# A token mixer, cosine attention and mixture of experts on one NeuronCore: pairs of heads attended two at a time, and the fillers of TensorE's order moved

## The reference, cut to what matters

```python
# token mixer, per sample: x is (F=64, L=256, H=4)
q, k, v = proj(Wq), proj(Wk), proj(Wv)             # (256, 256) each
ew = exp(w_bias * local_mask); ek = exp(k)
y = sigmoid(q) * (ew @ (ek * v)) / (ew @ ek)
h = layernorm(y @ out_w + out_b + flatten(x))
# attention over 257 tokens, 16 heads, DK = 16, DV = 64
t = layernorm(h)
q, k, v = l2norm(t @ Wq), l2norm(t @ Wk), l2norm(t @ Wv)    # per head
out = square(relu(q @ k.T)) @ v                    # per head
out = tanh(|out|) * out / |out|                    # per head and token
h = h + concat(out) @ Wout
```

## Time and profile before

| | |
|---|---|
| median of three runs | 3233.44 us (3223.12 to 3235.12) |
| profiled execution, its own time | 3228.84 us |
| its span in the profile | 3227.0 us |
| PE busy | 2987.7 us (93%) |
| DVE, ACT, POOL busy | 2108.6 (65%), 1431.1 (44%), 1150.4 us (36%) |
| loop of the 32 samples | about 100 to 1630 us of the span |

### The profile page before, as it was taken

The page is one execution under the profiler, slowest core; times in us unless marked ns, Lnnn a source line. Parts: engine busy times, 40 slices in busy tenths (PEclk is TensorE's granted clock), DMA queues, the critical chain, the costliest instruction groups (busy, mean ns, idle before and its releaser), DMA issues. The chain is left out here.

```text
span 3227.0 us, 67632 instructions
## 1 busy us (share of the span) xinstructions
PE 2987.7 (93%) x21936; PEld 2303.3 (71%) x21937; DVE 2108.6 (65%) x5558; ACT 1431.1 (44%) x2884; POOL 1150.4 (36%) x973
## 2 busy tenths in 40 slices
PE   3999999999999999999859999999999992999998
PEld 1677777777777777777537777777777761999997
DVE  4677777767777777776526777777777765444443
ACT  0444554554454455445404444444444442444443
POOL 3333433443443344344311222222222224444444
PEclk7999999999999999999969999999999995999999
DMA  3333442443343344234221111111111101444444
GB/s 82 92 87 73 101 99 66 95 104 75 81 104 88 72 101 103 64 92 104 49 51 31 37 49 42 36 52 41 37 52 39 39 31 46 73 75 78 76 78 67
DMA packets 161128, 223.14 MB, mean 69 GB/s; under 512 B 30305, under 2 KB 125730, under 8 KB 161074
## 3 DMA queue, kind: packets, MB, share of 16 engines
q1 hardware_dynamic: 135138, 187.50, 23.2%
q0 software_dynamic: 25936, 34.95, 6.9%
HBM read 125.26 MB, written 97.08 MB: 69 GB/s over the span
## 5 line engine op out<-in xcount | busy, mean ns | idle before, releaser
L66 POOL TENSOR_TENSOR vrn<-vsm,inv_root 128x16 f32<-128x16 f32 x64 | 247.1, 3862 | 282.1 <-DVE vsm L844 282.1
L673 ACT ACTIVATE R<-psA 128x1024 f32<-128x1024 f32 x256 | 262.5, 1025 | 167.9 <-PE psA L1158 164.3
L865 DVE TENSOR_TENSOR PR<-R 128x1024 f32<-128x1024 f32 x256 | 320.9, 1254 | 0.0
L2528 POOL DMA_INDIRECT out_rows<-e_y,e_dest x137 | 213.4, 1557 | 290.7 <-DMA out_rows<-e_y,e_dest 205.8
L1907 DVE TENSOR_REDUCE m_nm<-psC 128x4 f32<-128x1028 f32 (+1 forms) x256 | 239.4, 958 | 99.5 <-PE psC L2184 99.4
L1173 PE MATMUL psA<-PR,V 128*64 128x258 f32 x2048 | 283.2, 397 | 0.0
L1785 ACT ACTIVATE m_PT<-psC 128x770 f32<-128x770 f32 x256 | 194.1, 811 | 150.5 <-PE psC L2210 150.5
L678 ACT ACTIVATE oTs<-psA 128x258 f32<-128x258 f32 x256 | 99.2, 387 | 357.9 <-PE psA L1173 352.3
L1218 PE MATMUL psA<-wout,OT 128*128 128x256 f32 x1024 | 244.5, 382 | 0.4 <-DVE OT L907 0.4
L1704 POOL DMA_INDIRECT xg<-tn,idx x124 | 122.4, 987 | 335.5 <-DMA xg<-tn,idx 225.4
L1218 PEld LDWEIGHTS psA<-wout,OT 128*128 128x128 f32 x1024 | 188.5, 191 | 24.6 <-DVE OT L907 0.7
(11 more groups left out here) (423 smaller groups left out, 7774.4 us busy)
## 6 DMA issues: line engine op xcount, KB each, us to landing
ks<-kparts SPq DMA_DIRECT2D x256, 128.0 KB, 3.2
qs<-qparts SPq DMA_DIRECT2D x256, 128.0 KB, 3.6
e_x<-xg SPq DMA_DIRECT2D x143, 129.0 KB
xraw<-in_x SPq DMA_DIRECT2D x66, 256.0 KB
qparts<-qh SPq DMA_DIRECT2D x128, 128.0 KB, 2.4
kparts<-kh SPq DMA_DIRECT2D x64, 128.0 KB, 2.5
kparts<-kl SPq DMA_DIRECT2D x64, 128.0 KB, 2.4
qparts<-ql SPq DMA_DIRECT2D x64, 128.0 KB, 2.4
```

Of the source, the lines that this page charges most:

```text
L66: return pool.tensor_tensor(out, x, e.to_broadcast(list(out.shape)), ALU.pow)
L673: act.activation(R[:, p % 2].rearrange("p a t n -> p t a n"), ps[:, 0:2, :].rearrange("p t (a n) -> p t a n", a=2), ACT.Relu).then_inc(rel ...
L865: dve.tensor_tensor(PR[:, p % 2, :, :, 0:L], R[:, p % 2], R[:, p % 2], ALU.mult).then_inc(prob_done, 1)
L2528: pool.indirect_dma_start(out, bass.IndirectOffsetOnAxis(ap=dest[:, b % XD:b % XD + 1], axis=0), y[:, b % XD], None, compute_op=ALU.add).t ...
```

## The change

`attend` takes two pairs, `first` and `first + 1`: it waits until the outputs of the two pairs before are taken, adds the class part of both pairs, and then runs the matmuls of both, the second four behind a wait for the second pair's probabilities. So a sample has four visits in place of eight. The orders of TensorE, ACT and DVE are rewritten around that. POOL's and SP's are as before. No operation is added or taken away. DVE's lines have numbers lower by one than before, TensorE's lower by two up to `attend` and higher by one behind it, ACT's are as they were: `mixer_queries` is L1029, `mix_keys` L1043, `mixer_output` L1071, `sim` L1156, the class part L1167, the visit's matmuls L1174, `onm` L884, `mixed_rows` L783.

```diff
@@ attend, TensorE
-            def attend(i, d, p):
-                if p == 0:
+            def attend(i, d, first):
+                pairs = (first, first + 1)
+                if first == 0:
                     pe.wait_ge(p_ready, i + 1)
                     pe.wait_ge(v_ready, 2 * i + 2)
-                need(pe, o_sq, PAIRS * i + p - 1)
-                pe.wait_ge(prob_done, PAIRS * i + p + 1)
-                pe.matmul(ps[:, 2 + p % 2, 0:QCOLS], ...)
-                for t in range(LT):
...
-                last.then_inc(av_done, 1)
+                need(pe, o_sq, PAIRS * i + first)
+                for p in pairs:
+                    pe.matmul(ps[:, 2 + p % 2, 0:QCOLS], ...)
+                for p in pairs:
+                    pe.wait_ge(prob_done, PAIRS * i + p + 1)
+                    for t in range(LT):
...
+                    last.then_inc(av_done, 1)
@@ sample, DVE
                     denominators(j)
                     inverses(j, 0)
-                prob(i, d, 2)
                 if before:
                     output_scale(i - 1, 1 - d)
                 if more:
                     inverses(j, 1)
+                    mixed_rows(j)
+                prob(i, d, 2)
                 if before:
                     output_scale_turned(i - 1)
-                if more:
-                    mixed_rows(j)
+                prob(i, d, 3)
                 if before:
                     split_scale(i - 1)
-                prob(i, d, 3)
```

More of the change, by code:

```diff
@@ L703, in sample @@
                     take_outputs(i - 1, 1 - d, 7)
-                relu(i, 0)
                 if before:
                     sums_out(i - 1, 1)
+                relu(i, 0)
                 if more:
@@ L709, in sample @@
                 relu(i, 1)
-                take_outputs(i, d, 0)
                 relu(i, 2)
-                take_outputs(i, d, 1)
                 if before:
                     norm_tanh(i - 1)
+                take_outputs(i, d, 0)
+                take_outputs(i, d, 1)
                 relu(i, 3)
+                relu(i, 4)
                 take_outputs(i, d, 2)
-                relu(i, 4)
                 take_outputs(i, d, 3)
                 relu(i, 5)
-                take_outputs(i, d, 4)
+                relu(i, 6)
                 sums_out(i, 0)
@@ L725, in sample @@
                     queries(j)
-                    values(j, 0)
-                relu(i, 6)
-                if more:
-                    values(j, 1)
+                take_outputs(i, d, 4)
                 take_outputs(i, d, 5)
@@ L732, in sample @@
                 if more:
+                    values(j, 0)
+                    values(j, 1)
                     values(j, 2)
@@ L1160, in sim @@
                 last.then_inc(sim_done, 1)
-            def attend(i, d, p):
-                if p == 0:
+            def attend(i, d, first):
+                pairs = (first, first + 1)
+                if first == 0:
                     pe.wait_ge(p_ready, i + 1)
                     pe.wait_ge(v_ready, 2 * i + 2)
-                need(pe, o_sq, PAIRS * i + p - 1)
-                pe.wait_ge(prob_done, PAIRS * i + p + 1)
-                pe.matmul(ps[:, 2 + p % 2, 0:QCOLS], v.vcls3[:, p * P:(p + 1) * P], v.pcl[:, d, :], start=True,
-                          stop=False, skip_group_check=True)
-                for t in range(LT):
[L1171 to L1174, removed]
-                last.then_inc(av_done, 1)
+                need(pe, o_sq, PAIRS * i + first)
+                for p in pairs:
+                    pe.matmul(ps[:, 2 + p % 2, 0:QCOLS], v.vcls3[:, p * P:(p + 1) * P], v.pcl[:, d, :], start=True,
+                              stop=False, skip_group_check=True)
+                for p in pairs:
+                    pe.wait_ge(prob_done, PAIRS * i + p + 1)
+                    for t in range(LT):
+                        for hh in range(2):
+                            n = 2 * p + hh
+                            last = pe.matmul(ps[64 * hh:64 * hh + 64, 2 + p % 2, 0:QCOLS], V[:, d, t, n * DV:(n + 1) * DV],
+                                             PR[:, p % 2, hh, t, :], start=False, stop=True, skip_group_check=True)
+                    last.then_inc(av_done, 1)
             def head_sums(i, b):
@@ L1243, in sample @@
                 j = i + 1
-                sim(i, 0)
                 if more:
@@ L1250, in sample @@
                     mixer_keys(j, 0)
+                sim(i, 0)
                 if before:
@@ L1255, in sample @@
                 sim(i, 1)
-                attend(i, d, 0)
                 if more:
@@ L1261, in sample @@
                     mix_values(j)
-                attend(i, d, 1)
+                attend(i, d, 0)
                 if more:
@@ L1265, in sample @@
                 sim(i, 3)
-                attend(i, d, 2)
+                if more:
+                    mixer_output(j)
                 if before:
                     turn_scale(i - 1, more)
-                if more:
-                    mixer_output(j)
                 sim(i, 4)
+                attend(i, d, 2)
                 if before:
@@ L1282, in sample @@
                     project_outputs(i - 1, 2)
-                attend(i, d, 4)
+                sim(i, 6)
                 head_sums(i, 0)
@@ L1292, in sample @@
                     project_queries(j)
[L1293 to L1297, removed]
+                attend(i, d, 4)
                 sim(i, 7)
                 if more:
+                    project_values(j, 0)
+                    project_values(j, 1)
                     key_sums(j)
```

3 lines of the change are left out of this document (removed).

## The result

The changed kernel takes 3274.42 us (median of four runs, 3272.63 to 3279.87) against 3229.13 us of the kernel before on the same chip: a ratio of 1.0143, 95% interval 1.0117 to 1.0169. The forecast was 3278 us, slower. The profiled execution took 3274.26 us; the sum had said 3274 for it.

A forecast was written before the change was run, and what follows sets the result against it. TensorE was taken as the bound, 47.43 us a sample. New waits of 3.45 less gains of 1.94 give +1.51 us per sample, +45 over thirty; against the 3233.44 median, forecast 3278 us, range 3238 to 3312.

The forecast's parts named there:

- query sums directly before the queries: TensorE's mixer queries wait for DVE's q_lift, no longer covered: 0.55 us per sample, bounds 0.3 to 0.6.
- mix of keys: Without the first visit in front, it waits for ACT's exponentials: 0.65 us per sample, bounds 0 and 0.9.
- mixer output: Block L1071 waits for y_done, delayed by POOL's root ahead of the second inverse: 1.9 us per sample, bounds 0.9 to 2.3.
- first output projection: Little is left between it and the spread it needs, so it waits for DVE's L907: 0.35 us, 0 to 0.5.
- class products, behind the key norms: Key norms come 0.2 us before TensorE asks: no cost, up to 0.5 us if late.
- gains, visits and old waits: Fewer visits and class-row places save 1.25 us per sample, vanished old waits 0.69: together 1.94.
- The largest term: The mixer output's wait for y_done behind POOL's 5.42 us root: 1.9 us per sample.
- Rival C: Waits cost only their idle time, weight loads being pulled ahead: +0.47 us per sample, about 3247 us; chance 0.09.
- The 0.43 of waiting: Old order's first class row waits 0.43 us for the first probabilities; goes if the new place covers it.
- B: Faster: y_done comes in time for the mixer output, sample changes by -0.40 to -1.0 us, some 3210; chance 0.10.
- D: Slower still: the new hole lowers TensorE's clock, +1.13 us in each of thirty samples, 3310 us; chance 0.11.
- The lock between DVE and POOL: POOL's 16-row operation starting first might hold DVE's first probabilities: chain up to about 0.4 us longer, sum 12 us.

The follow-up runs named there:

- Experiments 1 and 5: On the changed kernel: 1 moves DVE's output_scale behind the mixed rows, 3244.19 us; 5 replaces POOL's root of the output norms by a multiplication, 3229.56 us.
- experiment 3: The changed kernel with ACT's exponential of the queries ahead of the first relu, behind a DMA wait: 3287.26 us, 1.0174 of the kernel before.

## Why the prediction was right

Term by term, in us per sample; the measured costs are the mean steps of the changed kernel less those of the same block with nothing to wait for:

| term | forecast | measured |
|---|---|---|
| query sums directly before the queries | 0.55 | 0.61 |
| mix of keys | 0.65 | 0.66 |
| mixer output | 1.9 | 1.84 |
| first output projection | 0.35 | 0.35 |
| third output projection | 0 | 0.18 |
| class products, behind the key norms | 0, up to 0.5 | 0.10 |
| gains, visits and old waits | -1.94 | -2.01 (the remainder) |
| sum | +1.51 | +1.73 |

*The largest term* held in its parts. From the end of the turned sums (L1191, 1032.99) osm ended 3.04 later, the root 8.53 and y_done 11.47, where the forecast had 3.04, 8.54 and 11.5; TensorE arrived after 9.97 (forecast 9.95). Experiments 1 and 5 take the root out in two ways, once by order and once by length, and the hole goes with it in both.

*The two small terms that failed* were wrong in their price, not in their place. The key norms were placed 0.2 before TensorE asks, and that is where they came:

```profile
1072.53 0.62 PE L1116 MATMUL psA<-wvh,xl 128*128 128x512 f32 x2
1073.02 1.09 PE L1135 MATMUL psA<-xT,wkc 128*80 128x256 f32 x4
...
1072.78 0.18 DVE L815 TENSOR_SCALAR km<-psA 128x32 f32<-128x32 f32 x1
```

They end at 1072.96, 0.19 before the block in front of the class products ends (1073.15), and the class products still take 0.96 for 0.86. "Nothing" was the wrong price for that. The third projection the forecast did not look at: it priced the first alone. The third waits for DVE's third scaling (L906), which stands in DVE's queue behind the first layer norm of the next sample and the statistics of the second; in the sample above it ended at 1054.63, 0.09 before TensorE was free. Its step is 1.91 for 1.73. Together 0.28, the whole excess of the waits.

*What a signal costs.* These rows give a price that the forecast had only for a signal that is late. Take how long before the end of the block in front DVE's result is finished, and what the block behind loses:

| block | finished before the end in front, us | lost, us |
|---|---|---|
| third projection, kernel before | 0.35 to 0.49 | 0 |
| class products, changed kernel | 0.19 | 0.09 |
| third projection, two kinds of samples | 0.18, 0.10 | 0.14, 0.22 |
| mixer output, experiment 1, two kinds of samples | 0.22, 0.11 | 0.10, 0.21 |
| mixer output, kernel before | 0.06 | 0.26 |
| first projection, changed kernel | -0.03 | 0.35 |
| mixer output, changed kernel | -1.50 | 1.82 |

For the output projections and the mixer output the two add up to 0.32 each time something is lost, for the class products, with 80 stationary columns, to 0.28. So a result has to be there about 0.3 us ahead of TensorE to cost nothing, and a block can lose up to 0.27 without showing any idle time. Where it does show some, the cost is more by 0.27 in the mix of keys, the mixer output and the first projection, and by 0.24 in the queries. The forecast was 0.26.

The page "TensorE: Matmul & The Clock Gate" of the Trainium skill, in the section "Architectural detail: the array is 16× 32×32, not 1× 128×128", says that weight loads can be pulled ahead of matmuls in flight. That did not shorten these waits. In the mixer output and the mix of keys the stationary operand is the late tile itself, so there was nothing to load; in the queries it is wq_bd, which is always there, and still the load starts at 1029.29, 0.11 behind the end of qm. Rival C has fallen.

*The gains*, -2.01 against -1.94, agree better than their parts. The visits are as forecast. The 0.43 of waiting in front of the first class row was read in one sample; over 25 the old kernel waited 0.28 there. What makes up for it was not in the sum: the old order's last similarity had a step of 0.81 in the mean, 0.66 without waits (TensorE stood idle 2.6 us in the 29 periods for the DMA of queries), and its last visit one of 1.09, 1.02 at the full clock.

*Where the total agreed by luck.* 29 periods give +50.1 us, 6 more than 29 times 1.51; the spans differ by 45.2, the 45 of the forecast. Before the first period the changed kernel gains 3.0 (144.49 against 147.50). The first similarity of sample 0 had waited 3.00 us for the DMA of its queries; it now stands behind the mixer's queries and keys and waits 0.74. From the last mark on, over samples 30 and 31, it loses 4.2, where 1.5 was forecast for sample 30 alone. The prediction had put sample 31, which has no mixer, at nothing; but there the turned scale now comes ahead of the third pair of heads and not behind it, and it waits for the same root. The first row is sample 0 in the kernel before, the second sample 31 in the changed one:

```profile
100.12 1.19 PE L1158 MATMUL psA<-qs,ks 128*128 128x512 f32 x2 [3.00 <-DMA qs<-qparts]
```

```profile
1633.07 0.69 PE L1200 MATMUL psA<-ident,osc 128*128 128x128 f32 x2 [4.81 <-DVE osc L893]
```

In the kernel before that second wait was 0.24. All that comes behind, which the change does not touch, took 6.1 us less in this execution; its largest stage takes 1058 to 1069 us over the eleven traces. So errors of +6, -3, +3 and -6 cancelled.

*Rivals.* B needed a signal 1.65 us earlier, and got none. D was not seen here: the loop's granted clock is 1.00, and the longest period is 49.24. But something like it was near: with a hole of 1.88 us in place of 1.54 to 1.63 (experiment 3) the clock fell in five of fifteen samples, at 1.7 us each and not the 1.13 taken.

*The lock between DVE and POOL*, left in the range, did not matter: POOL's 16-row operation ran at 1032.22 in 0.63 us, over by 1032.85, about 1 us before DVE's first probabilities. The class parts had ended earlier than forecast. In the kernel before the two had met in nearly every sample, and where POOL came first DVE's probabilities took 1.76 us and not 1.22: 0.5, a little more than the 0.4 of the forecast's upper bound.

## What to carry to other kernels

When work is taken from between a producer and its consumer, add up what the removed blocks had covered: four visits fewer saved about 2 us of TensorE's time and old waits and uncovered 3.7. In an in-order queue the position of the wait decides, not the position of the work: one wait for a 5.4 us root, put in front of an inverse, cost 1.1 to 1.3 of the 2.0 us gained, and moving four calls, without touching a matmul's count, turned 1.4% slower into 0.5% faster. A moved wait takes its followers along: with output_scale behind the mixed rows the largest hole closed, and 0.5 us came out at the two blocks that hang on output_scale, each to be found in the next trace. And "just in time" is late: a result finished 0.2 us before TensorE was free still cost 0.1, without any idle time in the trace.

## What the runs showed of the hardware

POOL's root of 16 columns takes 2.89 us alone, and 3.80 to 3.99 beside DVE. In the kernel before, DVE's scaling of the values, from SBUF to SBUF, had begun 0.17 us before the second root; in the changed kernel the root began 0.08 us ahead of it:

```profile
904.03 1.22 DVE L848 TENSOR_TENSOR V<-Vr,vc 128x1024 f32<-128x1024 f32 x1
904.20 3.80 POOL L66 TENSOR_TENSOR vrn<-vsm,inv_root 128x16 f32<-128x16 f32 x1 [0.23 <-DVE vsm L844]
```

```profile
1026.86 1.22 DVE L847 TENSOR_TENSOR V<-Vr,vc 128x1024 f32<-128x1024 f32 x1 [0.78 <-POOL vc L596]
1026.78 2.89 POOL L66 TENSOR_TENSOR vrn<-vsm,inv_root 128x16 f32<-128x16 f32 x1
```

The page "SBUF — State Buffer", section "SBUF: two separate sides", of the Trainium skill has whichever starts first keep the other out, for the whole instruction. Where DVE starts first these rows agree: the root lost 0.9 us to a DVE instruction that had about 1.05 left. Where the root starts first they do not: DVE's scaling, 0.08 us behind it, takes 1.22 us both times, though the root runs on for 2.8. Beside the root of 5.4 us DVE's probabilities take 1.22 too, in all 30 samples of the changed kernel's loop. A short operation of POOL does hold DVE: 0.08 us behind its squares (L577, 0.61 us) the same scaling takes 1.62, in each of 32 samples of either kernel. So here the measurement decides: a root in front is no reason to fear for DVE, DVE in front is one to fear for the root.

Where the two start 0.02 us apart, either may win. The first root, 0.02 ahead of DVE's probabilities, takes 3.99 us in nearly all samples of the changed kernel, and 2.89 in thirteen of 32 in the third experiment; where it wins, DVE's probabilities take 1.28 and not 1.22. The mean of vrn fell from 3862 to 3435 ns by the second root, and the class parts behind it came earlier by about 0.9 us.

The granted clock, by the records of these traces: in the changed kernel, with holes of 1.54 to 1.63 us, it stayed at 2.4 GHz in every period of the loop; in experiment 3 it fell to 1.2 GHz in none of the fifteen samples with a hole of 1.62 to 1.65 and in five of the fifteen with one of 1.87 or 1.88. And it is not holes alone: in the kernel before it fell twice, at 383.3 and 857.8 us, with no idle time on TensorE in the 10 us ahead.
